# Attention probabilities turned by the DMA engines instead of TensorE, with the order on four engines changed, in a fused cross-attention and routed feed-forward kernel

## The reference

```python
q, k, v = x @ Wq.T, context @ Wk.T, context @ Wv.T            # x is the layer norm of the input, 16 heads of 64
sim = einsum('bhid,bhjd->bhij', q, k) * SCALE
sim = where(tgt_mask == 0, neg, sim); sim = where(src_mask[:, None, :], sim, neg)
attn = softmax(sim, axis=-1)
x = input + einsum('bhij,bhjd->bhid', attn, v) @ Wo.T + bo
# then, on the layer norm z of x: shared relu net + the relu net of the expert with the larger gate score, added to x
```

## Time and profile before

| | before |
|---|---|
| median of 3 runs | 1855.86 us (1855.59 to 1860.28) |
| the profiled execution: its time | 1857.37 us |
| the profiled execution: its span | 1855.7 us |
| TensorE busy over the span | 1816.3 us (98%) |
| VectorE, ScalarE, GpSimd busy | 797.8 (43%), 820.8 (44%), 509.2 (27%) |
| L474, 256 transposes on TensorE | 33.4 us busy, 273 ns each |
| L464 and L485, the attention's matmuls | 171.0 and 174.4 us busy |
| DMA queue of SyncE, share of 16 engines over the span | 34.4% |
| SyncE in 200 to 450 us: wait at L407 (`turn_x`) for GpSimd L344 | 127.8 us in 22 waits |

### The profile page before, as it was taken

One profiled execution on the slowest core, in us unless ns is written; L12 is line 12 of the kernel. 1 busy time (PEld: TensorE's weight loads), 2 busy tenths in 40 slices (PEclk: granted clock), 3 DMA queues, 4 the chain that ended last, 5 costly groups with the idle time before them and its releaser, 6 DMA issues.

```text
span 1855.7 us, 33404 instructions
## 1 busy us (share of the span) xinstructions
PE 1816.3 (98%) x11516; PEld 1145.4 (62%) x11517; DVE 797.8 (43%) x1651; ACT 820.8 (44%) x1441; POOL 509.2 (27%) x475
## 2 busy tenths in 40 slices
PE   8989999999999999999999999999999999999997
PEld 6334444544566666666666666666666666666664
DVE  6987778777344333343433333222222222222222
ACT  4655555555333333334444444333333343333333
POOL 2047777777101111211100011312211221221210
PEclk9999999999999999999999999999999999999999
DMA  9246555655932332323444493921111122121100
GB/s 330 86 95 158 161 164 165 177 165 137 296 130 81 99 95 82 100 80 125 126 156 138 142 332 105 264 55 46 47 46 45 39 57 54 51 61 47 46 24 15
DMA packets 225955, 214.44 MB, mean 116 GB/s; under 512 B 126635, under 2 KB 168140, under 8 KB 225484
## 3 DMA queue, kind: packets, MB, share of 16 engines
q1 hardware_dynamic: 216924, 188.09, 34.4%
q0 software_dynamic: 8944, 25.19, 4.4%
HBM read 129.57 MB, written 59.02 MB: 102 GB/s over the span
## 4 chain that ended last, share of the span: by engine, by line
PE 88%; DVE 5%; POOL 2%; issue 2%; DMA 1%; ACT 1%; SPq 0%; POOLq 0%; DVEq 0%; ACTq 0%
PE pS L1081 36%; PE pP L1093 18%; PE pG L1093 9%; PE pO L1093 9%; PE pO L485 7%; PE banks_a L464 4%; PE pS L464 3%; DVE seen L799 2%; DVE room_w L819 1%; PE pP L474 1%; POOL room_b L659 1%; POOL room_b L654 1%; DMA e_split<-room_b 0%; POOL room_a L344 0%; PE banks_a L507 0%
## 5 line engine op out<-in xcount | busy, mean ns | idle before, releaser
L1081 PE MATMUL pS<-room_a,room_w 128*128 128x256 f16 (+1 forms) x6336 | 765.0, 271 | 1.5 <-issue 1.1
L1081 PEld LDWEIGHTS pS<-room_a,room_w 128*128 (+1 forms) x6336 | 611.2, 98 | 182.1 <-issue 10.2
L1112 DVE TENSOR_TENSOR room_a<-room_a 128x256 f16<-128x256 f32 (+1 forms) x528 | 237.6, 450 | 906.3 <-ACT room_a L1106 894.9
L1093 PE MATMUL pP<-room_w,room_a 128*128 (+1 forms) x1584 | 383.5, 379 | 0.1
L1104 ACT ACTIVATE room_a<-pS,room_b,sc 128x256 f32<-128x256 f32 (+1 forms) x272 | 151.7, 558 | 420.4 <-PE pS L1081 395.7
L1104 ACT ACTIVATE room_a<-pS,b1s,sc 128x256 f32<-128x256 f32 x256 | 144.2, 563 | 370.0 <-PE pS L1081 365.2
L1093 PEld LDWEIGHTS pP<-room_w,room_a 128*128 128x128 f16 x1584 | 154.8, 98 | 132.2 <-issue 0.7
L1093 PE MATMUL pG<-room_w,room_a 128*128 128x512 f16 (+1 forms) x768 | 207.6, 379 | 0.5 <-DVE room_a L1112 0.5
L1093 PE MATMUL pO<-room_w,room_a 128*128 128x512 f16 (+1 forms) x768 | 207.5, 379 | 0.0
L1128 POOL TENSOR_TENSOR room_a<-room_a,room_b 128x512 f32<-128x512 f32 x32 | 42.7, 1354 | 516.6 <-DVE room_a L1119 516.6
L485 PE MATMUL pO<-room_w,room_b 128*128 (+1 forms) x768 | 174.4, 384 | 7.6 <-DVE room_b L703 7.5
(11 more groups left out here) (180 smaller groups left out, 1540.8 us busy)
## 6 DMA issues: line engine op xcount, KB each, us to landing
room_b<-in_w SPq DMA_DIRECT2D x64, 512.0 KB, 5.0
e_split<-room_b SPq DMA_DIRECT2D x64, 256.0 KB
room_w<-e_split SPq DMA_DIRECT2D x8, 2048.0 KB
rows_room<-in_x SPq DMA_DIRECT2D x32, 256.0 KB, 3.1
room_a<-in_sw SPq DMA_DIRECT2D x32, 256.0 KB, 4.2
room_b<-in_x SPq DMA_DIRECT2D x32, 256.0 KB, 3.8
s_split<-room_a SPq DMA_DIRECT2D x64, 128.0 KB, 3.7
x_scratch<-room_b SPq DMA_DIRECT2D x32, 256.0 KB, 4.0
```

The lines of the kernel that those rows point to most:

```text
L1081: mm = q.matmul(self.pH[j % 2][:, 0:rows], w[:, k, j * P:(j + 1) * P], zt[:, u, k, 0:rows], start=(n == 0), stop=(n == 3 * KC - 1))
L1093: mm = q.matmul(self.pY[u][r][:, :], h[:, j % self.HR, r * P:(r + 1) * P], w[:, j, :], start=(j == 0 and n == 0), stop=(j == HC - 1 and n ...
L1112: q.tensor_tensor(self.hl[:, j % self.HR, 0:rows], self.hf[:, j % self.HR, 0:rows], self.hh[:, j % self.HR, 0:rows], ALU.subtract).then_in ...
```

## The change

- **TensorE**: `t_p` and the identity matrix are gone. `attend` waits for the DMA semaphore `pT_in` instead of VectorE's `pTl`.
- **ScalarE and VectorE**: `hi_p` and `lo_p` now take the unturned probabilities from `s` (on-chip memory, not PSUM) for tile i + 1, and write their two halves side by side into one tile `prs` (128 x 2048, 16-bit, a single buffer). Each stands last in its engine's iteration. `hi_p` waits until the transpose of the tile before has landed.
- **SyncE**: a new step `turn_p` of tile i + 1 at the end of each iteration turns `prs` by one DMA transpose of 16 blocks of 128 x 128 into `pT` (two buffers).
- **VectorE**: `dropped` behind `stats`; `gate`, `shifts2`, `shifts` and `pick` ahead of `sums`; `sums` directly ahead of `masked`.
- **GpSimd**: `low_w`, `norm`, `lo_z`, `sub` in this order instead of `norm`, `sub`, `low_w`, `lo_z`.
- The small tiles of the shared net are laid elsewhere in `room_b`, and VectorE waits at the start of the shared net until 31 `lo_z` are done.

```diff
+                    def turn_p(e, g, u):
+                        e.wait_ge(S["pl"], count(g, u))
+                        at_least(e, S["att"], count(g, u) - 2)
+                        e.dma_start(pT[:, u % 2, :, :], prs[:, :, :, :].rearrange("p l h k -> p (l h k)"), transpose=True).then_inc(S["pT_in", u % 2], 16)
...
                             step(sp, g, u, -2, store_z)
+                            step(sp, g, u, 1, turn_p)
                             if isinstance(g, int) and N * g + u == SUB - 2:
                                 load_next()
...
                     def attend(e, g, u):
-                        e.wait_ge(S["pTl"], count(g, u))
+                        e.wait_ge(S["pT_in", u % 2], dma_count2(g, u))
...
-                            for pt, f in ((pTh, fvh), (pTh, fvl), (pTl, fvh)):
-                                mm = e.matmul(pO[:, :], pt[:, q, :], f[:, bass.ds(b, 1), q, :],
+                            for c, f in ((q, fvh), (q, fvl), (PAIRS + q, fvh)):
+                                mm = e.matmul(pO[:, :], pT[:, u % 2, c, :], f[:, bass.ds(b, 1), q, :],
...
-                            if first_tile(g, u, 0):
-                                step(pe, g, u, 2, sim)
-                            step(pe, g, u, 0, t_p)
-                            if not first_tile(g, u, 0):
-                                step(pe, g, u, 2, sim)
+                            step(pe, g, u, 2, sim)
                             step(pe, g, u, 0, attend)
...
                     def hi_p(e, g, u):
-                        e.wait_ge(S["pT"], count(g, u))
-                        at_least(e, S["att"], count(g, u) - 1)
-                        e.activation(pTh[:, :, :], pP[:, :].rearrange("p (k n) -> p k n", k=PAIRS), ACT.Copy, scale=P_SCALE).then_inc(S["pTh"], 1)
+                        e.wait_ge(S["prob"], count(g, u))
+                        if u > 0:
+                            e.wait_ge(S["pT_in", (u - 1) % 2], dma_count2(g, u - 1))
+                        elif not isinstance(g, int) or g > 0:
+                            e.wait_ge(S["pT_in", 1], 32 * g)
+                        e.activation(prs[:, 0, :, :], s[:, u % 2, :, :], ACT.Copy, scale=P_SCALE).then_inc(S["ph"], 1)
...
-                            step(act, g, u, 0, hi_p)
                             step(act, g, u, 1, exp)
...
                                 step(act, g, u, 4, normal)
+                            step(act, g, u, 1, hi_p)
...
+                            step(pool, g, u, 2, low_w)
                             step(pool, g, u, 1, norm)
+                            step(pool, g, u, -1, lo_z)
                             step(pool, g, u, 2, sub)
-                            step(pool, g, u, 2, low_w)
-                            step(pool, g, u, -1, lo_z)
...
+                            step(dve, g, u, 1, sums)
                             step(dve, g, u, 2, masked)
...
+                            step(dve, g, u, 1, lo_p)
...
+        dve.wait_ge(z_done, SUB - 1)
         dve.tensor_scalar(rb1[:, :], b1e[:, :], 0.0, None, ALU.max).then_inc(S["rb1"], 1)
```

More of the change, by code:

```diff
@@ L247, in xattn_ffn @@
                         S[n, u] = a.enter_context(nc.semaphore(f"a_{n}{u}"))
-                for n in ("r_in", "sw_in", "sw_out", "xT_in"):
+                for n in ("r_in", "sw_in", "sw_out", "xT_in", "pT_in"):
                     for u in range(2):
@@ L276, in xattn_ffn @@
                 ri = take([2, HEADS])
-                pTh = take([PAIRS, P], F16)
-                pTl = take([PAIRS, P], F16)
+                pT = take([2, 2 * PAIRS, P], F16)
                 xr = take([2, DM])
@@ L282, in xattn_ffn @@
                 zs = take([2, 2 * DM], F16)
+                prs = take([2, HEADS, KEYS], F16)
                 st = sb("st", [P, 2, 6], F32, a)
@@ L913, in body @@
                             step(dve, g, u, -1, residual)
-                            step(dve, g, u, 0, lo_p)
-                            step(dve, g, u, 2, dropped)
                             if not early(g, u, 4):
@@ L920, in body @@
                             step(dve, g, u, -1, stats2_done)
-                            step(dve, g, u, 1, sums)
+                            step(dve, g, u, 2, dropped)
                             if not early(g, u, 4):
@@ L924, in body @@
                             step(dve, g, u, -1, aggregate2)
+                            step(dve, g, u, -1, add_eps2)
                             if not early(g, u, 4):
                                 step(dve, g, u, 4, add_eps)
-                            step(dve, g, u, -1, add_eps2)
+                            step(dve, g, u, -1, agg2_done)
+                            step(dve, g, u, -1, gate)
+                            step(dve, g, u, -1, shifts2)
+                            if not early(g, u, 4):
+                                step(dve, g, u, 4, shifts)
+                            step(dve, g, u, -1, pick)
                             if first_tile(g, u, 2):
                                 other_scales()
-                                step(dve, g, u, 4, shifts)
+                            step(dve, g, u, 1, sums)
                             step(dve, g, u, 2, masked)
-                            step(dve, g, u, -1, agg2_done)
-                            if not early(g, u, 4) and not first_tile(g, u, 2):
-                                step(dve, g, u, 4, shifts)
-                            step(dve, g, u, -1, shifts2)
-                            step(dve, g, u, -1, gate)
-                            step(dve, g, u, -1, pick)
+                            step(dve, g, u, 1, lo_p)
                     groups(dve, SUB // N, body, peel_last=1)
@@ L945, in xattn_ffn @@
                 el = take([2, 2, DM], F16)
-                brow = take([DM])
-                take([DM])
-                cacc = take([2, DM])
+                brow, cacc = room_b[:, 7264:7776], room_b[:, 8288:9312].rearrange("p (e n) -> p e n", n=DM)
+                take, late_take = carve(room_b[:, 6240:6752]), carve(room_b[:, 6752:7264])
                 inv = take([SLOT_SUBS])
@@ L951, in xattn_ffn @@
                 is0 = take([SLOT_TILES])
-                order = take([SLOT_SUBS])
-                iz = take([Net.N, Net.R], I32)
-                flags, needs = (take([SLOT_TILES], I32) for _ in range(2))
-                ir, io = (take([Net.N, Net.R], I32) for _ in range(2))
-                bsel = take([Net.N, HC])
+                order = late_take([SLOT_SUBS])
+                iz = late_take([Net.N, Net.R], I32)
+                flags, needs = (late_take([SLOT_TILES], I32) for _ in range(2))
+                ir, io = (late_take([Net.N, Net.R], I32) for _ in range(2))
+                bsel = late_take([Net.N, HC])
                 picks = (flags, needs, ir, io, bsel)
@@ L1015, with __init__ @@
     LAG = 2
-    def __init__(self, tag, count, sem, sc, ident, a1, a2, room, rows_room, banks, half=None):
-        self.tiles, self.ident, self.half = count, ident, half
+    def __init__(self, tag, count, sem, sc, a1, a2, room, rows_room, banks, half=None):
+        self.tiles, self.half = count, half
         self.a1, self.a2 = sc[:, a1:a1 + 1], sc[:, a2:a2 + 1]
```

36 lines of the change are left out of this document (11 added, 25 removed).

## The result

The changed kernel takes 1887.97 us in the median of 4 runs (1887.15 to 1889.53) against 1856.69 us (1855.59 to 1860.28, 4 runs of the kernel before): ratio 1.0166, 95% interval 1.0151 to 1.0181. It is slower by 31 us; the prediction was 1847 us, with 1866 as its upper end. The profiled execution took 1887.15 us, its span is 1885.4.

The account below looks back on a forecast made before the run. TensorE's 11.23 us a tile bounded the kernel, a two-tile ring of 11.32 a tile hidden behind it. Middle -17.7, start +5.5, end +3.4 gave -8.8 us, hence 1847 us; range 1835 to 1866.

Parts of the forecast that it names:

- `lo_p` 1.21 [...] taken as unchanged with its source on chip instead of in PSUM: Mid-loop term on VectorE: `lo_p` keeps its 1.21 us, part of the 10.01 us from `residual` to its end.
- Rival C: Mid-loop ring 0.4 to 0.6 us longer (`turn_p` 2.5, or `lo_p` slower on chip): 1853 us, chance 0.17.
- The ring: Mid-loop, `residual` through `lo_p`, `turn_p`, `turn_x` and `store_z`'s landing: 21.35 us for two tiles, 10.68 a tile.
- The middle without the stand-off: `attend` of tile 0 to tile 29: 310.1 us instead of 327.85, a gain of 17.7 us.
- The start: Before `attend` of tile 0: 3.8 us later, plus 1.7 for TensorE's slower clock; costs 5.5 us.
- The end: `attend` of tile 29 to the shared net: 1.7 us waiting for weights, 1.7 for the clock; costs 3.4 us.
- Rival D: Mid-loop, DMA engines join the ring through longer `turn_p` or later `store_z`: slower, 1862 to 1870 us, chance 0.18.
- its own 12 us for each microsecond: Rival D's price: each microsecond of longer `turn_p` or later `store_z` costs half of one in 24 tiles.
- Sum: Whole run: -17.7 middle, +5.5 start, +3.4 end, together -8.8 us.

Follow-up runs that it names:

- e2: Changed kernel with GpSimd's `sub` made to wait also for `lo_p` of the tile before; 1864.79 us, ratio 1.0043.
- e1: Changed kernel with `lo_p`'s second source a cleared PSUM tile instead of `prs`, high half not subtracted; 1856.70 us, ratio 0.9999.
- e11: Changed kernel with `lo_p`'s second source a cleared PSUM tile and no turn of the probabilities (`attend` reads ones); 1838.98 us, ratio 0.9904.
- e3: Kernel before with `lo_p` reading the probabilities from `s` in SBUF instead of their turned copy in PSUM; 1872.85 us, ratio 1.0086.
- e12: Kernel before, turn still on TensorE, with e4's order on VectorE, ScalarE and GpSimd (`hi_p` first, `lo_p` behind `residual`); 1856.70 us, ratio 0.9999.
- e4: Changed kernel, computation whole, with its operations in another order on VectorE, ScalarE and GpSimd; 1848.09 us, ratio 0.9955.
- e6: Changed kernel with GpSimd's order of before restored; 1903.06 us, ratio 1.0248.
- e9: e4 with SyncE's `store_x1` put ahead of `turn_x`; 1851.00 us, ratio 0.9970.

## Why the prediction was wrong, point by point

- **"`lo_p` 1.21 [...] taken as unchanged with its source on chip instead of in PSUM": the step that failed.** It measured 2.75 us. The operation has the same speed (e2), but with both sources in SBUF it and GpSimd's operations keep each other out, and the changed order put it 0.05 us behind the start of a 1.9 us `sub`. That costs 31.6 us of the middle (after against e1), and turns the forecast gain into the loss. The sentence was written as a duration; it should have been a question on what GpSimd does at that moment. Rival C named `lo_p` "slower on chip" and priced it at 0.4 to 0.6 us. The trace of before had the sign, in small, in the rows behind this list.
- **The ring.** I followed a ring of two tiles through SyncE. From `residual` to the end of `lo_p` I had 10.01; e1, where nothing stands, shows 9.99 us at the least (205.76 to 215.75) and 10.34 in the mean. But VectorE does the next `residual` right behind, so that stretch is a ring of one tile too. At 10.01 it lies under 10.68 and doesn't show; with 1.7 us more it is the longest. I never wrote down that it was within 0.7 us of binding.
- **The middle without the stand-off.** e1 has 317.6 us; I had 310.1. Of the 7.5 between, 1.8 are the slow clock of the first `attend` (1.6 in e1 itself), which the forecast booked in the start; 5.7 stay. The forecast's ring, read off in e1's trace in the mean of `residual` of tiles 3 to 25, is: to the end of `lo_p` 10.34 us (forecast 10.01), to the start of `turn_x` 1.98 (2.1), from there to `store_z` 5.32 (4.97), landing 4.08 (4.27), to `residual` 0.18 (nothing). That is 21.89 us instead of 21.35, 10.95 a tile instead of 10.68. So two terms were too small, VectorE's stretch by 0.33 and the one that I had kept "as now" by 0.35; in e11, without `turn_p`, the latter is 4.82, and the issue of `turn_x` is 1.24 us instead of 1.79. In VectorE's stretch a wait of `shifts` for GpSimd's L634 is new, 0.24 us in nearly every tile; the rest of its 0.33 stays open, and it isn't the transfers', as e11 has 10.31 there.
- **The start.** `attend` of tile 0 comes 4.2 us later behind `sim` (forecast 3.8), and at a lower granted clock takes 7.14 us instead of 5.35 (forecast 1.7 more): right, though TensorE stood idle for 9.25 us before it where I had 7.2.
- **The end.** 2.6 us (forecast 3.4): right in kind. The net waits for its weights, 2.37 us where I had 3.8; its first matmuls take 4.11 us as before, so the 1.7 us for the clock are not there. The slow stretches fall on `attend` of tiles 30 and 31.
- **Rival D** (SyncE and the DMA engines) had the right sign by the wrong cause: `turn_p` stayed under 2 us in the median and `store_z`'s landing at 4.2 us. Its prices don't follow from its own 12 us for each microsecond either: 2 us more give 1871 and 2.6 give 1878, not 1862 and 1870, and the range's upper end of 1866 stands for 1.6 us more.
- **Sum.** The profiled spans differ by +29.7 us where I had -8.8. The 38.5 us between are, up to rounding, 31.6 (stand-off), 5.7 (middle otherwise), 0.5 (start), -0.8 (end), 1.2 ahead of the loop and 0.4 behind it. The 1.2 isn't shown to be the change: that cut lies between 106.3 and 107.9 us in the twelve experiments, at 107.0 in e3 and 107.7 in e12, whose code up to there is that of before.

The sign in the trace of before: `dropped`, with both sources on chip, takes 0.21 us in the median (L769); here, beside `lo_x`, it takes 0.51, and its record ends 0.07 us behind `lo_x`'s:

```profile
114.05 1.16 POOL L344 TENSOR_TENSOR room_a<-room_a 128x512 f16<-128x512 f32 x1 [5.12 <-ACT room_a L547]
...
114.77 0.51 DVE L769 SCALAR_TENSOR_TENSOR room_a<-room_a 128x64 f32<-128x64 int32 x1
```

## What to carry to other kernels

When an edit moves a source of a VectorE operation from PSUM to SBUF, count how many sources are in SBUF then, and lay its place over GpSimd's timeline: two engines that never waited for each other can become one. A record that is longer than its twin's with no wait shown is the sign, and who started first tells, nearly always, who stands. And when a chain moves onto one engine, write down the ring of one tile on that engine beside the longer one, with the distance at which it binds.

## What the runs showed of the hardware

- The stand-off lasts until the other instruction ends, in both directions, and the loser's record counts it as busy: 2.94 us for 1.2 of work, 2.91 for 1.9, 2.14 for 1.16. In the changed kernel, e4 and e6, each `lo_p` that met a running operation ended 1.08 us after it, whether 0.7 or 1.86 us of it were left.
- It needs both sources of the VectorE instruction in SBUF: `masked` (L765), with one in PSUM and one in SBUF, takes 1.20 us at 315.53 beside GpSimd's `norm` at 315.69, which takes its usual 1.9; and in e1 `lo_p` with one source in PSUM takes 1.22 us beside a `sub` of 1.9.
- An issue that transposes eight blocks, 0.11 us behind one of sixteen, holds SyncE 1.78 us in the median instead of 1.24; the one of sixteen takes 1.56 to 3.06 us, 1.83 in the median. The shorter the first, the longer the second: in the median the pair takes 3.61 us. In e9, with a store and some 1.3 us in all between the two, the second is at 1.30; in e2 and e6, with 0.8 to 1.7 us, at 1.23.
- After 9.25 us of idleness TensorE's 24 matmuls took 7.14 us instead of 5.35. By stretch (busy us of PE, PEld, DVE, ACT, POOL, then granted clock, DMA share, GB/s) the clock granted there was 0.75, so part of it ran at the lower of the two levels, 1.2 GHz:

```profile
132.00:140.00 8.00, 7.62 (x27) 3.11 (x28) 4.78 (x4) 3.56 (x4) 5.65 (x3) 0.75 0.86 206
```
